# A windowed-attention block on one core: on-chip relayout by way of HBM, a new order of the passes, and residual sums of four groups on VectorE

## The reference

```
x = x + dwconv3x3(x) * s + b
x = x + ffn0(x)                       # 1x1 convs 64 -> 128 -> 64, relu, scale and bias
x = x + windowed_attention(x)         # 7x7 windows, 4 heads of 16, padded image
x = x + dwconv3x3(x) * s + b
x = x + ffn1(x)
```

## Time and profile before

| what | us |
|---|---|
| median of 3 runs (189.22 to 191.05) | 189.38 |
| the profiled execution, its own time | 190.28 |
| its span (first to last instruction) | 188.5 |
| PE busy in the span | 163.7 (87%) |
| DVE / ACT / POOL busy | 102.0 / 88.3 / 63.9 |
| mean granted TensorE clock | 0.946 |

### The profile page before, as it was taken

One profiled execution on the slowest core, in us unless ns is written; L12 is line 12 of the kernel. 1 busy time (PEld: TensorE's weight loads), 2 busy tenths in 40 slices (PEclk: granted clock), 3 DMA queues, 4 the chain that ended last, 5 costly groups with the idle time before them and its releaser, 6 DMA issues.

```text
span 188.5 us, 6709 instructions
## 1 busy us (share of the span) xinstructions
PE 163.7 (87%) x2840; PEld 79.9 (42%) x2840; DVE 102.0 (54%) x237; ACT 88.3 (47%) x183; POOL 63.9 (34%) x91
## 2 busy tenths in 40 slices
PE   6967959999999999999968899997939998799294
PEld 3311415454548465653737537644306441112141
DVE  1186323576766797987997988629151510013113
ACT  2055852868583846658553366252241354112112
POOL 3000205234463323629449268033073370300000
PEclk9999996999999999999996999999996999669969
DMA  5999998250000000000431412312334414433533
GB/s 149 291 301 233 214 220 165 69 96 2 3 3 3 3 3 3 3 3 3 98 69 32 97 39 62 79 30 72 70 97 96 111 42 98 102 93 82 161 129 111
DMA packets 17005, 16.68 MB, mean 89 GB/s; under 512 B 2128, under 2 KB 16720, under 8 KB 16848
## 3 DMA queue, kind: packets, MB, share of 16 engines
q1 hardware_dynamic: 16544, 15.74, 35.2%
q10 hardware_dynamic: 432, 0.52, 1.1%
HBM read 8.13 MB, written 2.10 MB: 54 GB/s over the span
## 4 chain that ended last, share of the span: by engine, by line
PE 34%; issue 18%; SPq 12%; POOL 11%; DVE 10%; ACT 6%; DMA 5%; POOLq 0%; DVEq 0%; ACTq 0%
SPq L307 12%; PE ps L648 9%; PE ps L674 4%; DMA wts<-in_weights 4%; PE ps L668 3%; POOL k L355 3%; DVE k L1025 3%; POOL y L374 3%; PE ps L755 3%; PE ps L717 2%; PE ps L732 2%; POOL qt L368 2%; PE ps L841 2%; DVE q L1032 1%; PE ps L797 1%
## 5 line engine op out<-in xcount | busy, mean ns | idle before, releaser
L648 PE MATMUL ps<-xc,dwf 96*32 96x480 f32 (+3 forms) x408 | 47.0, 601 | 5.8 <-DMA xc<-x 5.8
L648 PEld LDWEIGHTS ps<-xc,dwf 96*32 96x32 f32 x408 | 12.7, 118 | 33.0 <-issue 22.9
L368 POOL TENSOR_TENSOR qt<-q 128x512 f32<-128x512 f32 x8 | 10.3, 1286 | 36.2 <-ACT q L465 36.2
L431 ACT ACTIVATE hid<-ps,wts 128x512 f32<-128x512 f32 x28 | 17.7, 681 | 6.2 <-PE ps L668 6.2
L424 ACT ACTIVATE x<-ps,wts 128x512 f32<-128x512 f32 x15 | 10.2, 682 | 22.1 <-PE ps L648 22.1
L1095 DVE TENSOR_SCALAR x<-ps,bsum 128x512 f32<-128x512 f32 x7 | 5.2, 749 | 27.7 <-PE ps L674 27.7
L668 PE MATMUL ps<-x,w1s 64*128 64x512 f32 x60 | 16.9, 640 | 2.5 <-ACT x L424 2.2
L674 PE MATMUL ps<-hid,w2s 128*64 128x512 f32 x60 | 18.6, 667 | 0.1
L355 POOL TENSOR_TENSOR k<-k 128x640 f32<-128x640 f32 x8 | 12.3, 1539 | 13.8 <-ACT k L453 13.8
L717 PE MATMUL ps<-x,wts 64*64 64x512 f32 x32 | 10.0, 700 | 6.0 <-issue 2.3
L384 POOL TENSOR_TENSOR x<-xw,x 128x196 f32<-128x196 f32 x16 | 9.3, 601 | 17.3 <-ACT xw L525 10.9
(11 more groups left out here) (133 smaller groups left out, 278.3 us busy)
## 6 DMA issues: line engine op xcount, KB each, us to landing
xc<-in_x SPq DMA_DIRECT2D x16, 240.0 KB, 10.0
xc<-x SPq DMA_DIRECT2D x64, 60.0 KB, 2.0
xc<-in_x SPq DMA_DIRECT2D x8, 256.0 KB, 9.6
xc<-x SPq DMA_DIRECT2D x32, 64.0 KB, 2.0
out<-x SPq DMA_DIRECT2D x7, 256.0 KB, 2.5
tab<-in_tables SPq DMA_DIRECT2D x1, 1024.0 KB, 11.4
wts<-in_weights SPq DMA_DIRECT2D x1, 644.0 KB, 7.4
tap<-in_taps ACTq DMA_DIRECT2D x1, 210.0 KB, 4.0
```

The costliest lines, as they stand in the source:

```text
L368: eng.tensor_tensor(qt[:, g % QB, 0:GC], q2[:, g % 2, 0:GC], q1[:, :], ALU.mult).then_inc(qt_ready, 1)
L431: eng.activation(hid[:, m % 2, a, :], bank(P_H + a), ACT.Relu, bias=ww(f"fb1_{m // NG}")).then_inc(h_ready[a], 1)
L648: last = eng.matmul(out_ps[32 * q:32 * q + 32, :, :, to], dwf[:, s, q % 2, i, :], src[:, :, :, of], start=(i == 0), stop=False, skip_group ...
```

## The change

The change moves steps in the programs of all engines and replaces three mechanisms.

1. **Relayout by HBM.** A DRAM tensor `mid` takes x3 in one DMA; SP waits for it, then `rows(mid, 8+c)` loads xc in three DMAs. Stores of out stand before groups 5, 6, 7 (out groups 0, 1, 2) and behind them.
2. **Residual sums.** third(0) to third(3) stay on ACT and POOL, with two buffers of xw. third(4) to third(7) are VectorE's, from the projection's bank.
3. **Operands in PSUM.** The reciprocal in `ratios` (from f = 3) and the last masked sum in `take_y` are written to free PSUM columns instead of SBUF.
4. **Order.** Passes 1..4 on TensorE begin with ffn1(n), conv(n+1); pass 5 begins with ffn1, attend; window_conv(5) moves from pass 10 to pass 9; the tail is rewritten; conv(15) is issued in two halves around ffn1(14). ACT and VectorE are reordered to match; POOL runs y_sum(5) before any third of the tail; hidden(12)'s second half goes to VectorE; slot 13 uses the banks P_A.

```diff
+    mid = nc.dram_tensor("mid", [B, C, HW, HW], F32).ap()
...
-        xw = sb("xw", 128, GP, PX)
+        xw = sb("xw", 128, 2, GP, PX)
...
-        FM_SLOT = {5: 1, 6: 2, 9: 3, 10: 5}
+        FM_SLOT = {5: 1, 6: 2, 9: 3}
+        FM_LAST = 5
...
             for c in range(NG):
-                if 4 <= c < 6:
-                    eng.wait_ge(x2_ready, NG + c - 3)
...
+                if c >= 5:
+                    eng.wait_ge(x2_ready, NG + c - 4)
+                    store(c - 5, slice(0, GP))
                 eng.wait_ge(x3_ready, c + 1)
+                eng.dma_start(by_channel(mid)[c], x3[:, c % 2, :].rearrange("p (j n) -> p j n", j=GP)).then_inc(mid_out, 16)
+                eng.wait_ge(mid_out, 16 * (c + 1))
                 eng.wait_ge(conv_ps, NG + c - NB + 1)
-                rows_on_chip(c)
+                rows(mid, NG + c)
...
+                if n == 11:
+                    y_sum(5)
+                if 0 <= n - 7 < 4:
                     third(n - 7)
-                if n >= 6:
+                if 6 <= n < 11:
                     y_sum(n - 6)
...
             y_sum(6)
             y_sum(7)
-            third(5)
-            third(6)
-            third(7)
...
+            first(0)
             eng.wait_ge(u_ready, 1)
             eng.activation(sp[:, 3, :], sp[:, 2, :], ACT.Ln).then_inc(ln_ready, 1)
-
-            first(0)
...
             for n in range(1, 5):
                 if n >= 2:
+                    k_square(n - 2)
+                hidden(n)
...
+                if n >= 2:
                     q_sixth(n - 2)
...
                 first(n + 1)
                 if n >= 2:
                     root(n - 2)
-                second(n)
+                take_v_rest(n - 1)
+                q_square(n - 1)
                 if n >= 2:
                     take_q_norms(n - 2)
-                take_v_rest(n - 1)
+                take_v_full(n - 1)
+                second(n)
...
-            def kv_rest(g):
+            def kv_rest(g, n):
                 eng.wait_ge(x2_ready, g + 1)
+                if n < 5:
+                    eng.wait_ge(h_ready[0], n + 1)
+                    eng.wait_ge(h_ready[1], n + 1)
...
-                    eng.wait_ge(xw_ready, c)
+                    if c > 4:
+                        eng.wait_ge(x3_ready, c)
...
             for n in range(1, 5):
+                ffn1(n, n)
+                conv(n + 1, n + 1)
                 query(n - 1, n)
                 kv_full(n - 1, n)
-                ffn1(n, n)
...
             project(6, 13)
+            turn_y(7, 13)
             ffn2(11)
-            turn_y(7, 13)
+            project(7, 13)
             conv(12, 13)
-            project(7, 13)
+            conv(13, 14)
             ffn1(12, 13)
-            conv(13, 14)
+            ffn1(13, 14)
             ffn2(12)
-            ffn1(13, 14)
+            ffn2(13)
             conv(14, 15)
-            ffn2(13)
+            conv(15, 16, slice(0, 1))
             ffn1(14, 15)
-            conv(15, 16)
+            conv(15, 16, slice(1, 2))
+            ffn1_half(0)
             ffn2(14)
-            ffn1_half(0)
...
+                part = rat[:, 0, :]
+                if f >= 3:
+                    eng.wait_ge(z_ps, f - 2)
+                    part = bank(P_A)[:, 7 * VC:7 * VC + 20]
...
+            def third(c):
+                eng.wait_ge(pj_ps, c + 1)
+                eng.wait_ge(x3_ready, c)
+                eng.wait_ge(mid_out, 16 * (c - 1))
+                dst, src = x3[:, c % 2, :], bank(proj_bank(c))
+                for j in range(GP):
+                    for wx in range(2):
+                        at = PX * j + 98 * wx
+                        eng.scalar_tensor_tensor(natural(dst, j)[:, 0:14, WR * wx:WR * wx + WR],
+                                                 src[:, at:at + 98].rearrange("p (h w) -> p h w", w=WR), projc[:, 0:1],
+                                                 x2[:, c, j, 98 * wx:98 * wx + 98].rearrange("p (h w) -> p h w", w=WR), ALU.add, ALU.add)
+                for j in range(GP):
+                    at = PX * j + WIN
+                    eng.scalar_tensor_tensor(natural(dst, j)[:, :, 14:16], src[:, at:at + 32].rearrange("p (h w) -> p h w", w=2),
+                                             projc[:, 0:1], x2[:, c, j, WIN:WIN + 32].rearrange("p (h w) -> p h w", w=2), ALU.add, ALU.add)
...
+                last.then_inc(x3_ready, 1)
...
+                rest = zr[:, :, 0, :]
+                link(eng.scalar_tensor_tensor(rest, zr[:, :, 2, :], cc("mask3")[:, 2:3], yr[:, :, :], ALU.mult, ALU.add))
...
             take_y(6)
+            third(4)
             second(10)
             take_y(7)
+            third(5)
+            third(6)
             second(11)
+            third(7)
+            hidden_b(12)
+            hidden_b(13)
             second(12)
-            hidden_b(13)
             second(13)
```

More of the change, by code:

```diff
@@ L426, in hidden @@
             def hidden(m):
-                for a in range(2 if m < 13 else 1):
+                for a in range(2 if m < 12 else 1):
                     eng.wait_ge(h_ps, 2 * m + a + 1)
@@ L430, in hidden @@
                         eng.wait_ge(f_ps, m - 1)
-                    eng.activation(hid[:, m % 2, a, :], bank(P_H + a), ACT.Relu, bias=ww(f"fb1_{m // NG}")).then_inc(h_ready[a], 1)
+                    eng.activation(hid[:, m % 2, a, :], bank(hidden_bank(m) + a), ACT.Relu, bias=ww(f"fb1_{m // NG}")).then_inc(h_ready[a], 1)
             def take_v_full(g):
@@ L607, in _ @@
                     eng.wait_ge(f_ps, LAST - 1)
-                eng.activation(hid[:, 1, 0, PX * j:PX * j + PX], bank((P_H, P_A)[j])[:, 0:PX], ACT.Relu, bias=ww("fb1_1"))\
+                eng.activation(hid[:, 1, 0, PX * j:PX * j + PX], bank((P_A, P_H)[j])[:, 0:PX], ACT.Relu, bias=ww("fb1_1"))\
                    .then_inc(h_ready[0], 1)
@@ L914, in _ @@
                     q_norms(n - 2)
+                ffn2(n)
                 if n == 1:
                     setup_pads()
+                if n >= 3:
+                    key_value_full(n - 3, n)
             for n in range(5, 11):
                 m = conv_of(n)
-                if m is not None and n > 5:
-                    conv(m, n)
-                if n - 3 < NG:
+                if n == 5:
+                    ffn1(m, n)
+                    attend(n - 5, n)
                     key_value_full(n - 3, n)
-                if n >= 7:
-                    project(n - 7, n)
-                if n == 5:
-                    attend(n - 5, n)
                     window_conv(FM_REST_SLOT[n], n)
-                if m is not None:
-                    ffn1(m, n)
-                if n > 5:
+                else:
+                    if m is not None:
+                        conv(m, n)
+                    if n - 3 < NG:
+                        key_value_full(n - 3, n)
+                    if n >= 7:
+                        project(n - 7, n)
+                    if m is not None:
+                        ffn1(m, n)
                     attend(n - 5, n)
@@ L944, in _ @@
                     window_conv(FM_REST_SLOT[n], n)
+                    turn_y(n - 6, n)
                 if n - 1 < NG:
-                    kv_rest(n - 1)
+                    kv_rest(n - 1, n)
                 if n - 3 < NG:
@@ L1206, in _ @@
                     scale_taps(1)
+            take_kv_full(1)
             for n in range(5, 11):
```

169 lines of the change are left out of this document (82 added, 87 removed).

## The result

| | us |
|---|---|
| changed kernel, median of 4 runs (179.58 to 184.52), beside the prediction | 182.56 |
| kernel before, median of 4 runs (189.22 to 191.05) | 189.85 |
| ratio after to before, with its 95% interval | 0.948 [0.938, 0.959] |
| changed kernel again, 6 runs (177.98 to 183.64); before there, 11 runs | 178.99; 188.68 |
| and a second time, 6 runs (178.52 to 184.56); before there, 11 runs | 181.14; 190.76 |

The ratios here compare only the executions within 1.5% of the fastest of their kernel, so they differ a little from the ratios of the medians. Faster by about 5%: 7.3 us between these medians, 9.0 to 9.8 by the ratios of the three sets; forecast was 13.3. In this set the runs of the changed kernel lie 4.9 us apart and those of before 1.8; in the later sets both kernels spread by 5.7 to 8.1.

A forecast was written before the change was run, and what follows sets the result against it. The end was set by x3(5)'s readiness, three groups of SP's transfers and the work behind the last. Tail 8.2 + middle 3.3 + opening 1.8 = 13.3 off 190.28 = 177.0; median 0.9 lower, 176.1; range 168 to 184.

The forecast's parts named there:

- The tail: From conv(10)'s start to the end: 48.1 us for 56.3, so 8.2 us less.
- x3(5) ready at t = 14.5: Group 5's residual sum ready 14.5 us after conv(10)'s start (t = 0), where it was at 20.2.
- The eight ops of third: VectorE's eight unlinked scalar_tensor_tensor ops of third(5), taken at 1.5 us; at most 2.2, at start-to-start pace 1.3.
- The write: One DMA of a group's x3 to mid in HBM, shaped like the stores of out: 2.5 us to landing.
- The period: Time from one group's relayout to the next, back to back on SP's queue: 6.95 us, against 8.1 before.
- The middle: Stretch conv(7) to conv(10): 0.9 from moving window_conv(5), 2.2 to 2.5 from PSUM operands; together 3.3 us less.
- holes of 1.25 leave the clock alone: In the middle, the hole before query(7) shrinks to about 1.1 us, too short to bring half clock behind it.
- The opening: conv(0) to conv(7): filled holes save some 5 us, waits on ACT cost 3.3, leaving 1.8 less; bounds 5 and -4.
- (1): Rival: the last transfers hide, a write passing the reads, period 4.5 us, conv(15) not waiting; 169 us, chance 0.18.
- (2): Rival: ACT paces the opening, its four waits 2 us or more with half clock each pass; 182 us, chance 0.18.
- (3): Rival: the trip by HBM is slower, 14 us a period, losing once a period is over 11.4; 197 us, chance 0.04.
- (4): Rival: VectorE's third saves nothing, 2.9 us as before; 177.5 us, chance 0.55 together with the main case.

The follow-up runs named there:

- e5_on_chip: Changed kernel with the relayout SBUF to SBUF again, twelve copies a group on SP, no trip through HBM; 190.80 us, ratio 1.004 to the kernel before.
- e9_again2: The changed kernel as it is, run and profiled again; 181.14 us, ratio 0.953 to the kernel before.
- e12_ratios_sbuf: Changed kernel with only the ratios' reciprocal back in SBUF, the division's last masked sum still in PSUM; 185.79 us, ratio 0.981 to the kernel before.
- e4_act_order: Changed kernel with ACT's exchange undone: q_square ahead of take_v_full again in passes 5 to 8; 180.56 us, ratio 0.956 to the kernel before.
- e8_sbuf_operands: Changed kernel with both the ratios' reciprocal and the division's last masked sum back in SBUF; 186.06 us, ratio 0.983 to the kernel before.
- e11_combo_pool: Changed kernel with out stores behind the last reads, take_yt(3) ahead of take_q_norms(7), POOL issuing groups 5 to 7's writes to HBM; 175.91 us, ratio 0.929.
- e6_opening_old: Changed kernel with passes 1 to 4 and the start of pass 5 in the old order on all engines; 183.56 us, ratio 0.957 to the kernel before.

## Why the prediction was right, and where it was not

The time (182.56, then 178.99 and 181.14, for 176.1) lies in the range, the sign is right, and so is the place of most of the gain. The gain itself is 9.5 us for 13.3, and what is missing is the middle's. By its steps:

- **The tail, 8.2 us less: right**, 8.2 to 8.4 in three profiles. The hole of 3.17 us until POOL's y_sum is gone. x3(5) ready at t = 14.5: its write is issued at 14.8. The eight ops of third, 1.5 us: 1.63 (third(4), 141.42 to 143.05 on VectorE); these rows answer to the earlier trace rows:

```profile
141.42 0.99 DVE L1123 SCALAR_TENSOR_TENSOR x<-ps,projc,x 128x98 f32<-128x98 f32 x4
...
142.80 0.25 DVE L1130 SCALAR_TENSOR_TENSOR x<-ps,projc,x 128x28 f32<-128x28 f32 x1
```

  Four unlinked ops (none waits for the one before) of 312 ns each take 0.99 together, so the start-to-start pace of unlinked ops was the right choice and 359 ns apiece the wrong one. The write, 2.5 us: 2.6 in the median, but 4.8 and 4.2 for groups 6 and 7, which are issued behind reads. The period, 6.95: 6.5 to 6.8. The estimate by the Trainium skill (DMA: Bandwidth & Descriptors, Anatomy of one DMA) gave 6.3; that section is about DMAs issued by GpSimd, and these are SP's. One hole of 4 before conv(15): 4.06, with the clock down behind it; a second one of 1.3 before conv(13) was not forecast. That conv(15) starts within 0.5 us of the forecast (t = 36.1 to 36.4 for 36.55) is partly luck: the reads of group 7 are issued 1.0 to 1.2 us earlier than reckoned (30.6 to 30.8 for 31.8) and take 5.4 to 5.7 us for 4.75.
- **The trip through HBM carries the gain: right**, and more so than the text said. The prediction gave 5.7 us of the 8.2 to x3(5) being ready earlier. e5_on_chip has the same order and sums (its copies of group 5 start at t = 17.9 for 20.2) and gains nothing by them.
- **The middle, 3.3 us less: wrong in three steps.**
  - *The clock.* The forecast had "holes of 1.25 leave the clock alone", read off a single hole of one execution. In the changed kernel holes of 0.67 to 1.0 us stand before conv(8) and conv(9), and in some executions half clock follows: the middle is 2.9 us longer in one profile and 1.6 shorter in two. Executions of 183.2 to 184.6 us have a mean clock of 0.951 to 0.963, all others 0.978 to 0.990, so much of the spread is likely this; which conv paid is known only for the profiled ones.
  - *The size.* Even where no clock is lost (e9_again2), the way from conv(7) to conv(8) is 1.2 us shorter for the 2.2 to 2.5 forecast, and from there to conv(10) 0.4 for 0.9.
  - *The place.* That a PSUM operand frees VectorE of waiting on POOL is right (0.17 for 0.95). But it is not what shortens the hole before query(7), which starts as early without it (e12_ratios_sbuf). It shortens kv_full's wait; the 5.4 us of that run are this wait, the half clock behind it and the unexplained part. The hole before query(7) did shrink (2.17 to 1.42); ACT's exchange is worth 0.2 of that (1.66 in e4_act_order), and no run assigns the rest. Of the two places for the operand, the division is worth nothing that can be told. Without the ratios' operand the middle is 53.6 us, 3.3 longer than the old one; 2.45 of these are conv(8) at half rate, and whether the new order of pass 7 and on costs something itself is not shown.
- **The opening, 1.8 us less: a near number by luck.** 2.3 is seen against the one profile of before, but it is 1.7 of half rate behind a hole that the old order has in either case and 0.6 between the first two convs; filling the holes, from which the forecast began, is worth nothing (71.41 and 71.39). The waits on ACT came (0.28, 0.25, 0.38 and 0.48 us in e8_sbuf_operands, whose opening is the changed one), half as long as forecast. Others were not forecast: two of 0.71 us, where ffn1(4) and ffn1(5) wait for VectorE's kvm. The passes are no shorter, so TensorE's order does not bound them; what does was not tried.
- **Rivals.** (1), hidden transfers, did not occur: conv(15) waits 4.1. On SP a write behind reads takes 3.7 to 4.8 us to land, and SP issues a group's write only when it is through with the group before; in e11_combo_pool POOL issues the writes, and conv(15) finds its data. (Its sum, 17 + 9 + 4.75, is 30.75, not 30.6, which changes nothing.) (2) fell: no wait on ACT near 2 us. (3) fell: a period of 6.5 to 6.8 for the 11.4 needed. (4) fell: 1.63 us for 2.9.
- **The sum** adds parts that are not additive: taken back one at a time (difference of the ratios times the set's median before), the relayout is worth 10 us, the ratios' operand 5.4, the third 3.4, and the whole 9.5. That a part taken back leaves its wait on the path, whatever the others have won, would explain it, and e5_on_chip is such a case; for the other two it is argued.

## What to carry to other kernels

Price a relayout by issues as much as by bytes: twelve 60 KB copies from one queue took 8.4 to 9.2 us a group, a write and three reads through HBM 6.5 to 6.8, and with the writes issued by another engine the last group's no longer waited for SP to be through with the group before. Give a small VectorE op that sits on the path an operand in PSUM when GpSimd works beside it. And where TensorE has holes of about 1 us, take the profile of several executions before a gain or loss of 2 us is given to an edit, and see whether the half rate falls in front of a wait, where it was free, or behind the last one, where it was paid.

## What the runs showed that was not expected

- The same hole has two prices. Behind 2.33 us the query took 1.12 us in the profile of before and 0.65 in e6_opening_old; behind 0.67 and 0.79 us conv(8) took 4.67 in one execution of the changed kernel and 2.68 in another. Convs with half clock took up to 5.13 us, 2.45 more.
- A write beside reads is slow on either queue: group 6's write on POOL's is issued at 150.16 and the reads that wait for it at 154.59, 4.4 us; on SP's, right behind the reads of group 5, it takes 4.8 (153.95 to 158.77 in the first profile). Group 5's write, with no reads in front of it, lands in 2.7.
